# Second attention of a two-layer transformer kernel: PSUM banks shared out anew between two score passes

## The chip, the cores and the metric

The kernel runs on one core of a Trainium2 chip. It is one launch, and the metric is the device time of that launch in microseconds (us), taken as the median of several runs. The engines are TensorE (PE, with its weight loads in a row of their own, PEld), VectorE (DVE), ScalarE (ACT), GpSimd (POOL) and the queue of SyncE (SP), which issues most transfers.

## The reference, cut to what matters

The input is 16 sequences of 512 rows with 128 features. The layers are feed-forward, first attention, feed-forward, second feed-forward kind, second attention, second feed-forward kind. Only the second attention is touched by the change:

```python
B, L, C = x.shape            # 16, 512, 128
H = 16; D = C // H           # 16 heads of 8
qkv = (x @ w_qkv).reshape(B, L, 3, H, D).transpose(2, 0, 3, 1, 4)
q, k, v = (qkv[0], qkv[1], qkv[2])
q = _apply_rope(q, cos, sin)
k = _apply_rope(k, cos, sin)
attn = jnp.einsum('bhqd,bhkd->bhqk', q, k) * D ** (-0.5)
attn = jax.nn.softmax(attn, axis=-1)
out = jnp.einsum('bhqk,bhkd->bhqd', attn, v)
return out.transpose(0, 2, 1, 3).reshape(B, L, C) @ w_proj + b_proj
```

## The kernel before

A tile is one sequence: 512 rows, held as BLK = 4 blocks of 128 rows. The second attention (`attention1` on each engine, phase 4) computes the scores twice.

**Pass 1** (L2029, `pass1`) computes scores with the queries of one block as stationary operand and all 512 keys as moving operand: one 128x512 matmul for each of 4 query blocks of each of 16 heads. VectorE takes the negated maximum of each row from the PSUM bank (L1594, `maxima`). The maxima of a group of four heads are transposed (L2095, `shifted`) and added to the queries (L1600), so that the second pass gives scores with the row maximum already taken off.

**Pass 2** (L2040, `pass2`) computes the same scores transposed. One step deals with key block `h % 4` of the four heads of group `h // 4`: four 128x512 matmuls, one for each head `j` of the group. ScalarE takes the exponential out of PSUM into `prob` (L1019, `exps`). Then `values` (L2053) multiplies the exponentials with the values, four heads side by side in the array, accumulating in bank OB.

Pass 1 runs AHEAD = 5 heads before pass 2. A tile is 16 steps of h, each written out in the code of every engine (`step`), and there are 16 tiles, 256 steps in all. Nothing is reordered at run time: each engine executes its own list in order, and semaphores join the lists. `s1` counts matmuls of pass 1, `qmax` maxima, `st` finished matmuls of pass 2 and `prob` exponentials.

**TensorE's step** h before the change is: pass 2 for heads 0 and 1; `early_work`; pass 1 for block 2; pass 2 for heads 2 and 3; pass 1 for block 3; `values` of step h-1; `pass1_ahead`, which is pass 1 for blocks 0 and 1 of the next head; `late_work`. Early work is four 128x128 matmuls in steps 0, 3, 7, 11 and 15. Late work is eight 128x128 matmuls in steps 0 and 9 (L2069, L2087), three 128x512 matmuls in steps 1 and 3 (L1750 to L1752), and four 128x128 matmuls in steps 7, 8, 11, 12 and 13 (L2062, L2081). Steps 2, 4, 5, 6, 10, 14 and 15 have none. The first tile has none in steps 7 to 10 either.

**ScalarE's step** h is: `o_raw` in steps 1, 5, 9 and 13; a copy of rotated queries or keys (`qk_hl<-rope`) in steps 5 and 7; the exponentials of heads 0 and 1; two copies in step 0 and one in steps 1 and 9; the exponentials of heads 2 and 3. **VectorE's step** h is: two maxima; other work of that step (rotary products, `q_sh`, normalising the output); two maxima.

**The banks of PSUM** before the change: pass 1 uses banks 0 and 1 in turn (PASS1 + b % 2), each read by one VectorE instruction of 512 columns. Pass 2 uses banks 2 to 5 (PASS2 + j), and one ScalarE instruction reads two of them, 1024 columns. Bank 6 is OB, and bank 7 (MISC) serves everything else.

SyncE reloads `k_pad` for a group of the next tile after pass 2 has used it for the last time (L571, counted in `st`).

Of the kernel before, what the change touches and what calls it, by code (L numbers as in the profile page):

```python
# [7 lines left out]
ALU = mybir.AluOpType  # L8
# [122 lines left out]
def macaron(nc, x_in, w, const, out):  # L131
# [9 lines left out]
    with whole:  # L141
# [253 lines left out]
        PASS1, PASS2, OB, MISC = 0, 2, 6, 7  # L395
# [20 lines left out]
        def _(sp):  # L416
# [149 lines left out]
            def load_keys(t, g, again):  # L566

                if g == 0:
                    pass_wait(sp, sig(4, "k_out"), t * 48 + 64)
                if again:  # L570
                    pass_wait(sp, sig(4, "st"), t * 2 * HEADS - 2 * HEADS + 8 * g + 8)  # L571
                else:
                    pass_wait(sp, sig(4, "k_zero"), g + 1)
                for j in range(HPG):
                    sp.dma_start(k_pad[32 * j:32 * j + 3 * HD + 1, HPG * g + j, :].bitcast(F32), k_dram[HPG * g + j])\
                      .then_inc(sig(4, "k_pad"), 16)
# [40 lines left out]
            sp.wait_ge(sig(4, "st"), (TILES - 1) * 2 * HEADS + HEADS)  # L617
# [249 lines left out]
        def _(act):  # L867
# [135 lines left out]
            def attention1():  # L1003
# [12 lines left out]
                def exps(t, h, half):  # L1016
                    act.wait_ge(sig(ph, "st"), t * 2 * HEADS + 2 * h + half + 1)
                    b0 = PASS2 + 2 * half
                    act.activation(prob[:, h % HP, 2 * half:2 * half + 2, :], ps[:, b0:b0 + 2, :], ACT.Exp,  # L1019
                                   scale=SCALE).then_inc(sig(ph, "prob"), 1)  # L1020
# [70 lines left out]
        def _(dve):  # L1091
# [495 lines left out]
            def attention1():  # L1587
                ph = 4

                def maxima(t, g, j, blocks=range(BLK)):  # L1590
                    for b in blocks:
                        dve.wait_ge(sig(ph, "s1"), (t * GROUPS + g) * 16 + 4 * j + b + 1)
                        c = 32 * j + 3 * HD
                        dve.tensor_reduce(shift[:, g % 2, b, c:c + 1], wide(PASS1 + b % 2), AXX,  # L1594
                                          ALU.max, negate=True).then_inc(sig(ph, "qmax"), 1)
# [151 lines left out]
        def _(pe):  # L1747
# [266 lines left out]
            def attention1():  # L2014
# [6 lines left out]
                def pass1(t, g, j, blocks=range(BLK)):  # L2021
# [4 lines left out]
                    for b in blocks:  # L2026
                        if not (isinstance(t, int) and t == g == 0 and 4 * j + b < 2):
                            pe.wait_ge(sig(ph, "qmax"), (t * GROUPS + g) * 16 + 4 * j + b - 1)
                        pe.matmul(wide(PASS1 + b % 2), q_st[:, g % 2, b * P:b * P + P], k_pad[:, HPG * g + j],  # L2029
                                  start=True, stop=True).then_inc(sig(ph, "s1"), 1)  # L2030

                def pass2(t, h, half, first=False):

                    g, kb = h // HPG, h % HPG
                    if kb == 0 and half == 0:
                        pe.wait_ge(sig(ph, "qsh_sb"), t * GROUPS + g + 1)
                    if not first:
                        pe.wait_ge(sig(ph, "prob"), t * 2 * HEADS + 2 * h - 1 + half)
                    for j in (2 * half, 2 * half + 1):
                        last = pe.matmul(wide(PASS2 + j), k_pad[:, HPG * g + j, kb * P:kb * P + P],  # L2040
                                         q_sh[:, g % 2], start=True, stop=True)
                    last.then_inc(sig(ph, "st"), 1)

                def values(t, h, p):

                    g, kb = h // HPG, h % HPG
                    pe.wait_ge(sig(ph, "prob"), t * 2 * HEADS + 2 * h + 2)
# [112 lines left out]
                def step(t, p, h, more, before=None):  # L2160
                    first = h == 0 and before is None
# [3 lines left out]
                    pass2(t, h, 0, first)  # L2165
                    early_work(t, p, h, more, before)
                    if scores:
                        pass1(t1, g, j, (2,))
                    pass2(t, h, 1, first)
                    if scores:  # L2170
                        pass1(t1, g, j, (3,))
                    if h > 0:
                        values(t, h - 1, p)
                    elif before is not None:
                        values(before, HEADS - 1, 1 - p)
                    pass1_ahead(t, h + 1, more)
# [110 lines left out]
```

## Time and profile before

| | |
|---|---|
| median of 3 runs | 2481.73 us (2479.38 to 2483.67) |
| profiled execution, its own time | 2477.91 us |
| its span | 2476.0 us |
| PE busy | 2236.7 us, 90% of the span |
| DVE busy | 1986.3 us, 80% |
| ACT busy | 1298.4 us, 52% |
| POOL busy | 1024.6 us, 41% |
| L1594, maxima on DVE | 1024 instructions, 685 ns each |
| L1019, exponentials on ACT | 512 instructions, 1024 ns each |
| second attention, first to last matmul of its own | about 1126 to 2064 us of the span |

Busy time of PE is the sum of stretches in which a matmul is recorded as running. Matmuls are pipelined: a 128x512 matmul is recorded with some 0.39 us, while the next starts 0.23 us after it. So how fast PE goes is read from the starts of consecutive matmuls, not from their durations.

### The profile page before, as it was taken

How to read it: one execution, taken by the hardware profiler on the slowest of the kernel's cores; microseconds unless marked ns; L12 is line 12 of the kernel's file. 1: busy time of each engine (PE TensorE's matmuls, PEld its weight loads, DVE VectorE, ACT ScalarE, POOL GpSimd, SP SyncE). 2: the span in 40 equal slices, each digit the busy share in tenths (PEclk: the TensorE clock that was granted, in tenths of full speed). 3: DMA queues.
4: the chain of work that ended last, by engine and by line, in shares of the span. 5: the costliest groups of instructions: out<-in, count | busy, mean ns of one | idle time of the engine just before them, and what ended most of it. 6: DMA issues, size and time to landing. Idle time of an engine off the chain costs nothing.

```text
span 2476.0 us, 33777 instructions
## 1 busy us (share of the span) xinstructions
PE 2236.7 (90%) x11138; PEld 1544.6 (62%) x11138; DVE 1986.3 (80%) x4646; ACT 1298.4 (52%) x1907; POOL 1024.6 (41%) x953
## 2 busy tenths in 40 slices
PE   4499588779599999977999999999999999999999
PEld 3377366557377777764555555555555556777777
DVE  6588588768488888867888888888888886888887
ACT  1088333278444444433666666666666665444444
POOL 6646445536545655552211122212222203555554
PEclk9999666589789999996999999999999999999999
DMA  7243211144188887852222222222222206787887
GB/s 184 80 156 125 41 35 39 44 154 150 49 188 173 175 183 162 183 125 56 79 72 69 71 65 69 68 65 70 68 76 71 80 29 138 163 186 168 183 182 155
DMA packets 146489, 274.14 MB, mean 111 GB/s; under 512 B 21055, under 2 KB 24138, under 8 KB 146070
## 3 DMA queue, kind: packets, MB, share of 16 engines
q1 hardware_dynamic: 129942, 242.61, 41.1%
q0 software_dynamic: 16384, 29.46, 5.6%
q8 instruction: 89, 1.46, 0.3%
q14 instruction: 74, 0.61, 0.1%
HBM read 212.92 MB, written 54.65 MB: 108 GB/s over the span
## 4 chain that ended last, share of the span: by engine, by line
PE 40%; DVE 7%; DMA 5%; ACT 2%; issue 2%; SPq 0%; POOL 0%; DVEq 0%; ACTq 0%
PE ps L2029 12%; PE ps L2053 10%; PE ps L2040 9%; DMA gate_rows<-gates_dram 4%; DVE m L1429 2%; PE ps L1750 2%; DVE shift L1594 2%; PE ps L1752 2%; PE ps L1751 2%; PE ps L2062 1%; ACT hi L869 1%; PE ps L2095 1%; DMA gates_dram<-gateT 1%; DVE gate L1384 1%; PE ps L1764 1%
## 5 line engine op out<-in xcount | busy, mean ns | idle before, releaser
L1594 DVE TENSOR_REDUCE shift<-ps 128x1 fp32r<-128x512 f32 x1024 | 665.8, 685 | 132.9 <-PE ps L2029 127.2
L1019 ACT ACTIVATE prob<-ps 128x1024 f32<-128x1024 f32 x512 | 511.2, 1024 | 309.1 <-PE ps L2040 303.1
L869 ACT ACTIVATE hi<-m 128x512 fp32r<-128x512 f32 x512 | 319.0, 631 | 427.1 <-DVE m L1429 427.0
L707 POOL TENSOR_TENSOR lo<-m,hi 128x512 fp32r<-128x512 f32 x256 | 349.1, 1368 | 389.0 <-ACT hi L869 388.9
L2029 PE MATMUL ps<-k_pad,q_st 128*128 128x512 f32 x1024 | 405.2, 438 | 14.6 <-DVE shift L1594 7.2
L1429 DVE SCALAR_TENSOR_TENSOR m<-ps,gate_rows 128x512 f32<-128x512 f32 x512 | 334.8, 680 | 91.4 <-PE ps L1752 52.7
L2029 PEld LDWEIGHTS ps<-k_pad,q_st 128*128 128x128 f32 x1024 | 180.7, 190 | 271.1 <-DVE shift L1594 190.9
L2040 PE MATMUL ps<-q_sh,k_pad 128*128 128x512 f32 x1024 | 330.2, 404 | 0.0
L2053 PE MATMUL ps<-prob,v_cols 128*32 128x512 f32 x2048 | 272.7, 605 | 0.4 <-ACT prob L1019 0.4
L1096 DVE TENSOR_TENSOR lo<-m,hi 128x512 fp32r<-128x512 f32 x256 | 220.4, 861 | 16.8
L1750 PE MATMUL ps<-hi,vals_hl 128*128 128x512 f32 x512 | 211.1, 412 | 5.2 <-DVE lo L1096 4.5
L1750 PE MATMUL ps<-xnT_hl,keys_hl 128*128 128x512 f32 x512 | 210.0, 410 | 0.9 <-DVEq L382 0.9
L1751 PE MATMUL ps<-xnT_hl,keys_hl 128*128 128x512 f32 x512 | 204.2, 399 | 0.0
L1752 PE MATMUL ps<-xnT_hl,keys_hl 128*128 128x512 f32 x512 | 203.6, 398 | 0.0
L1752 PE MATMUL ps<-hi,vals_hl 128*128 128x512 f32 x512 | 203.1, 397 | 0.0
L1751 PE MATMUL ps<-lo,vals_hl 128*128 128x512 f32 x512 | 202.5, 395 | 0.0
L2040 PEld LDWEIGHTS ps<-q_sh,k_pad 128*128 128x128 f32 x1024 | 184.8, 189 | 27.0 <-ACT prob L1019 1.2
L785 POOL DMA_INDIRECT y_dram<-yb_rows,y_to x152 | 161.4, 1062 | 54.2 <-issue 54.2
L869 ACT ACTIVATE xnT<-ps 128x512 f32<-128x512 f32 x96 | 56.7, 590 | 225.1 <-PE ps L1757 121.2
L639 POOL TENSOR_SCALAR var_eps<-meanvar 128x4 f32<-128x4 f32 x48 | 11.2, 233 | 359.7 <-DVE meanvar L1653 279.0
L1096 DVE TENSOR_TENSOR g_lo<-g,g_hi 128x512 fp32r<-128x512 f32 x152 | 107.1, 705 | 35.5 <-ACT g_hi L869 30.5
L1750 PEld LDWEIGHTS ps<-hi,vals_hl 128*128 128x128 f32 x512 | 96.9, 189 | 41.0 <-DVE lo L1096 16.8
(215 smaller groups left out, 3847.9 us busy)
## 6 DMA issues: line engine op xcount, KB each, us to landing
gate_rows<-gates_dram SPq DMA_DIRECT2D x254, 512.0 KB, 12.0
w_blk<-w_dram SPq DMA_DIRECT2D x38, 514.5 KB, 3.7
q_st<-q_dram SPq DMA_DIRECT2D x64, 256.0 KB, 2.7
k_pad<-k_dram SPq DMA_DIRECT2D x256, 50.0 KB
k_dram<-qk_hl SPq DMA_DIRECT2D x48, 256.0 KB, 4.9
q_dram<-qk_hl SPq DMA_DIRECT2D x48, 256.0 KB, 3.0
x_blk<-sorted_x SPq DMA_DIRECT2D x38, 258.0 KB, 3.7
rope<-rope POOLq DMA_DIRECT2D x64, 128.0 KB, 3.3
```

Of the source, the lines that this page charges most:

```text
L707: pool.tensor_tensor(m["lo"][:, s], m["m32"][:, s], m["hi"][:, s].bitcast(F32), ALU.subtract).then_inc(sig(ph, "lo_pool"), 1)
L869: return act.activation(o, i, ACT.Copy)
L1019: act.activation(prob[:, h % HP, 2 * half:2 * half + 2, :], ps[:, b0:b0 + 2, :], ACT.Exp, scale=SCALE).then_inc(sig(ph, "prob"), 1)
L1096: return dve.tensor_tensor(o, a, b, ALU.subtract)
L1429: dve.scalar_tensor_tensor(out=m["m32"][:, fb % RING1], in0=wide(h1_bank[fb]), scalar=0.0, in1=m["gate_rows"][p][:, fb], op0=ALU.max, op1= ...
L1594: dve.tensor_reduce(shift[:, g % 2, b, c:c + 1], wide(PASS1 + b % 2), AXX, ALU.max, negate=True).then_inc(sig(ph, "qmax"), 1)
L1750: pe.matmul(dst, w_hi, x_hi, start=start, stop=False)
L1751: pe.matmul(dst, w_hi, x_lo, start=False, stop=False)
L1752: return pe.matmul(dst, w_lo, x_hi, start=False, stop=stop)
L2029: pe.matmul(wide(PASS1 + b % 2), q_st[:, g % 2, b * P:b * P + P], k_pad[:, HPG * g + j], start=True, stop=True).then_inc(sig(ph, "s1"), 1)
L2040: last = pe.matmul(wide(PASS2 + j), k_pad[:, HPG * g + j, kb * P:kb * P + P], q_sh[:, g % 2], start=True, stop=True)
L2053: last = pe.matmul(ps[rows(j), OB, :], v_cols[p][:, kb, HPG * g + j], prob[:, h % HP, j], start=(kb == 0), stop=(kb == BLK - 1))
```

## The change

Pass 1 gets four banks, 0 to 3, one for each query block (PASS1 + b). VectorE reads two neighbouring banks in one instruction and writes two maxima, so there are 512 instructions of 1024 columns instead of 1024 of 512. Pass 1 waits once for each pair of blocks: the pair may be written when the same pair of the previous head has been read. Pass 2 gets two banks, 4 and 5 (PASS2 + j % 2), where it had four. ScalarE reads one bank in each instruction, so there are 1024 exponentials of 512 columns instead of 512 of 1024. Each matmul of pass 2 for head j waits until the exponential two places before it has been taken, and `st` and `prob` now count single matmuls and single exponentials. TensorE's step changes its order: pass 1 for blocks 2 and 3 follow one another, and pass 2 for heads 2 and 3 moves behind `values`. SyncE's waits on `st` are rescaled and stand at the same point of the work.

```diff
-        PASS1, PASS2, OB, MISC = 0, 2, 6, 7
+        PASS1, PASS2, OB, MISC = 0, 4, 6, 7
...
                 def exps(t, h, half):
-                    act.wait_ge(sig(ph, "st"), t * 2 * HEADS + 2 * h + half + 1)
-                    b0 = PASS2 + 2 * half
-                    act.activation(prob[:, h % HP, 2 * half:2 * half + 2, :], ps[:, b0:b0 + 2, :], ACT.Exp,
-                                   scale=SCALE).then_inc(sig(ph, "prob"), 1)
+                    for j in (2 * half, 2 * half + 1):
+                        n = t * 4 * HEADS + 4 * h + j
+                        act.wait_ge(sig(ph, "st"), n + 1)
+                        act.activation(prob[:, h % HP, j, :], wide(PASS2 + j % 2), ACT.Exp,
+                                       scale=SCALE).then_inc(sig(ph, "prob"), 1)
...
                 def maxima(t, g, j, blocks=range(BLK)):
-                    for b in blocks:
-                        dve.wait_ge(sig(ph, "s1"), (t * GROUPS + g) * 16 + 4 * j + b + 1)
+                    for b in blocks[0::2]:
+                        dve.wait_ge(sig(ph, "s1"), (t * GROUPS + g) * 16 + 4 * j + b + 2)
                         c = 32 * j + 3 * HD
-                        dve.tensor_reduce(shift[:, g % 2, b, c:c + 1], wide(PASS1 + b % 2), AXX,
-                                          ALU.max, negate=True).then_inc(sig(ph, "qmax"), 1)
+                        dve.tensor_reduce(shift[:, g % 2, b:b + 2, c], ps[:, PASS1 + b:PASS1 + b + 2, :], AXX,
+                                          ALU.max, negate=True).then_inc(sig(ph, "qmax"), 2)
...
                     for b in blocks:
-                        if not (isinstance(t, int) and t == g == 0 and 4 * j + b < 2):
-                            pe.wait_ge(sig(ph, "qmax"), (t * GROUPS + g) * 16 + 4 * j + b - 1)
-                        pe.matmul(wide(PASS1 + b % 2), q_st[:, g % 2, b * P:b * P + P], k_pad[:, HPG * g + j],
+                        n = (t * GROUPS + g) * 16 + 4 * j + b
+                        if n >= 4 and b % 2 == 0:
+                            pe.wait_ge(sig(ph, "qmax"), n - 2)
+                        pe.matmul(wide(PASS1 + b), q_st[:, g % 2, b * P:b * P + P], k_pad[:, HPG * g + j],
...
-                def pass2(t, h, half, first=False):
+                def pass2(t, h, heads):
...
-                    if not first:
-                        pe.wait_ge(sig(ph, "prob"), t * 2 * HEADS + 2 * h - 1 + half)
-                    for j in (2 * half, 2 * half + 1):
-                        last = pe.matmul(wide(PASS2 + j), k_pad[:, HPG * g + j, kb * P:kb * P + P],
-                                         q_sh[:, g % 2], start=True, stop=True)
-                    last.then_inc(sig(ph, "st"), 1)
+                    for j in heads:
+                        n = t * 4 * HEADS + 4 * h + j
+                        if n >= 2:
+                            pe.wait_ge(sig(ph, "prob"), n - 1)
+                        pe.matmul(wide(PASS2 + j % 2), k_pad[:, HPG * g + j, kb * P:kb * P + P],
+                                  q_sh[:, g % 2], start=True, stop=True).then_inc(sig(ph, "st"), 1)
...
-                    pass2(t, h, 0, first)
+                    pass2(t, h, (0, 1))
                     early_work(t, p, h, more, before)
                     if scores:
-                        pass1(t1, g, j, (2,))
-                    pass2(t, h, 1, first)
-                    if scores:
-                        pass1(t1, g, j, (3,))
+                        pass1(t1, g, j, (2, 3))
                     if h > 0:
                         values(t, h - 1, p)
                     elif before is not None:
                         values(before, HEADS - 1, 1 - p)
+                    pass2(t, h, (2, 3))
                     pass1_ahead(t, h + 1, more)
                     late_work(t, p, h, more, before)
```

TensorE's list before the change, steps 4 and 5 of a tile in the middle of the phase (L2040 is pass 2, L2029 pass 1, L2053 `values`; the brackets name the semaphores waited for):

```order
L2040 MATMUL ps<-q_sh,k_pad 128x512 [waits prob_4,qsh_sb_4]
L2040 MATMUL ps<-q_sh,k_pad 128x512
L2029 MATMUL ps<-k_pad,q_st 128x512 [waits qmax_4]
L2040 MATMUL ps<-q_sh,k_pad 128x512 [waits prob_4]
L2040 MATMUL ps<-q_sh,k_pad 128x512
L2029 MATMUL ps<-k_pad,q_st 128x512 [waits qmax_4]
L2053 MATMUL ps<-prob,v_cols 32x512 [waits prob_4]
L2053 MATMUL ps<-prob,v_cols 32x512 x3
L2029 MATMUL ps<-k_pad,q_st 128x512 [waits qmax_4] x2
L2040 MATMUL ps<-q_sh,k_pad 128x512 [waits prob_4]
L2040 MATMUL ps<-q_sh,k_pad 128x512
```

The same place of the changed kernel, where the lines are L2043, L2031 and L2055 in the same order of meaning:

```order
L2043 MATMUL ps<-q_sh,k_pad 128x512 [waits prob_4,qsh_sb_4]
L2043 MATMUL ps<-q_sh,k_pad 128x512 [waits prob_4]
L2031 MATMUL ps<-k_pad,q_st 128x512 [waits qmax_4]
L2031 MATMUL ps<-k_pad,q_st 128x512
L2055 MATMUL ps<-prob,v_cols 32x512 [waits prob_4]
L2055 MATMUL ps<-prob,v_cols 32x512 x3
L2043 MATMUL ps<-q_sh,k_pad 128x512 [waits prob_4] x2
L2031 MATMUL ps<-k_pad,q_st 128x512 [waits qmax_4]
L2031 MATMUL ps<-k_pad,q_st 128x512
L2043 MATMUL ps<-q_sh,k_pad 128x512 [waits prob_4] x2
```

Pass 2 for heads 2 and 3 has moved behind `values`, so that two matmuls of pass 1 stand between it and the next step's pass 2, and each matmul of pass 2 now has a wait for an exponential. Before, a bank of pass 2 was written again only a whole step later.

ScalarE's list before the change, from step 1 of a tile to step 7:

```order
L869 ACTIVATE v_cols<-ps 128x64x8 [waits v_4]
L1019 ACTIVATE prob<-ps 128x1024 [waits st_4] x7
L869 ACTIVATE o_raw<-ps 128x512 [waits pv_4]
L869 ACTIVATE qk_hl<-rope 128x512 [waits k_out_4,rope_sum_4]
L1019 ACTIVATE prob<-ps 128x1024 [waits st_4] x4
```

And of the changed kernel:

```order
L869 ACTIVATE v_cols<-ps 128x64x8 [waits v_4]
L1020 ACTIVATE prob<-ps 128x512 [waits st_4] x14
L869 ACTIVATE o_raw<-ps 128x512 [waits pv_4]
L869 ACTIVATE qk_hl<-rope 128x512 [waits k_out_4,rope_sum_4]
L1020 ACTIVATE prob<-ps 128x512 [waits st_4] x8
```

The places of the other ScalarE work are the same; each exponential has become two, each with its own wait.

## Rows read from the trace of the kernel before

**Rows 1.** Busy time by stretch: start:end, length, PE, PEld, DVE, ACT, POOL, clock, DMA.

```profile
1000.00:1100.00 100.00, 92.93 (x415) 72.44 (x414) 79.16 (x174) 43.39 (x75) 51.35 (x42) 0.98 0.73 152
1115.00:1146.00 31.00, 16.79 (x33) 8.52 (x33) 21.21 (x33) 1.88 (x2) 8.25 (x10) 0.50 0.13 42
1166.00:2043.00 877.00, 872.35 (x4856) 493.64 (x4856) 750.50 (x1375) 564.66 (x644) 176.66 (x177) 1.00 0.25 68
```

**Rows 2.** Groups of instructions, 1166 to 2043 us: busy, mean ns, idle before.

```profile
L1594 DVE TENSOR_REDUCE shift<-ps 128x1 fp32r<-128x512 f32 x983 | 639.2, 686 | 124.1 <-PE ps L2029 118.5
L1019 ACT ACTIVATE prob<-ps 128x1024 f32<-128x1024 f32 x492 | 491.5, 1024 | 276.7 <-PE ps L2040 271.1
...
L2029 PEld LDWEIGHTS ps<-k_pad,q_st 128*128 128x128 f32 x984 | 170.8, 188 | 249.3 <-DVE shift L1594 176.4 <-issue 51.1
```

**Rows 3.** Timeline of PE, steps 4 and 5 of one tile: start, duration, instruction.

```profile
1447.37 0.39 PE L1750 MATMUL ps<-xnT_hl,w_qk 128*128 128x512 f32 x1
...
1448.07 0.62 PE L2040 MATMUL ps<-q_sh,k_pad 128*128 128x512 f32 x2
1448.53 0.40 PE L2029 MATMUL ps<-k_pad,q_st 128*128 128x512 f32 x1
...
1449.22 0.40 PE L2029 MATMUL ps<-k_pad,q_st 128*128 128x512 f32 x1
1449.55 1.06 PE L2053 MATMUL ps<-prob,v_cols 128*32 128x512 f32 x8
1450.54 0.72 PE L2029 MATMUL ps<-k_pad,q_st 128*128 128x512 f32 x2
1451.11 0.63 PE L2040 MATMUL ps<-q_sh,k_pad 128*128 128x512 f32 x2
1451.82 0.50 PE L2029 MATMUL ps<-k_pad,q_st 128*128 128x512 f32 x1
1452.16 0.62 PE L2040 MATMUL ps<-q_sh,k_pad 128*128 128x512 f32 x2
...
1454.55 0.63 PE L2040 MATMUL ps<-q_sh,k_pad 128*128 128x512 f32 x2
...
1457.92 0.39 PE L2040 MATMUL ps<-q_sh,k_pad 128*128 128x512 f32 x1
```

**Rows 4.** Timelines of DVE, PEld and ACT at the same steps.

```profile
1451.07 0.69 DVE L1594 TENSOR_REDUCE shift<-ps 128x1 fp32r<-128x512 f32 x1 [0.66 <-PE ps L2029]
...
1451.82 0.19 PEld L2029 LDWEIGHTS ps<-k_pad,q_st 128*128 128x128 f32 x1 [0.52 <-DVE shift L1594]
...
1448.72 1.94 ACT L1019 ACTIVATE prob<-ps 128x1024 f32<-128x1024 f32 x2 [2.03 <-PE ps L2040]
```

**Rows 5.** Shapes on ACT, whole span: busy, mean ns of one.

```profile
L896 ACT ACTIVATE g<-ps,w_blk 128x512 f32<-128x512 f32 x152 | 104.4, 687 | 25.7 <-PE ps L1752 24.2
...
L869 ACT ACTIVATE xnT_hl<-ps 128x512 fp32r<-128x512 f32 x102 | 60.1, 589 | 40.8 <-PE ps L1819 40.8
...
L869 ACT ACTIVATE o_raw<-ps 128x512 f32<-128x512 f32 x64 | 38.7, 605 | 2.6 <-PE ps L2053 1.9
```

**Rows 6.** Chain of waits, two pieces of late work: start, length, what.

```profile
1476.05 0.44 PE ps L2062 x4
...
2041.05 0.89 PE ps L2087 x8
```

**Rows 7.** Chain of waits, last steps of the phase: start, length, what.

```profile
2050.82 0.92 PE ps L2040 x4
2051.74 1.00 PE ps L2053 x8
2052.73 0.59 PE ps L2062 x4
2053.32 0.93 PE ps L2040 x4
```

**Rows 8.** ACT in step 5 (start, length), and a wait (total, times, longest).

```profile
1451.17 0.62 ACT L869 ACTIVATE qk_hl<-rope 128x512 fp32r<-128x512 f32 x1
...
ACT qk_hl L869 <- DMA rope<-rope: 31.9, 14, 2.6
```

More of the change, by code:

```diff
@@ L570, in load_keys @@
                 if again:
-                    pass_wait(sp, sig(4, "st"), t * 2 * HEADS - 2 * HEADS + 8 * g + 8)
+                    pass_wait(sp, sig(4, "st"), t * 4 * HEADS - 4 * HEADS + 16 * g + 16)
                 else:
@@ L615, in store @@
                 sp.dma_start(ov[:, bass.ds(t, 1)], xs[:, bass.ds(t, 1)]).then_inc(stored, 16)
-            sp.wait_ge(sig(4, "st"), (TILES - 1) * 2 * HEADS + HEADS)
+            sp.wait_ge(sig(4, "st"), (TILES - 1) * 4 * HEADS + 2 * HEADS)
             gates(TILES, 0)
@@ L2026, in pass1 @@
                     for b in blocks:
-                        if not (isinstance(t, int) and t == g == 0 and 4 * j + b < 2):
-                            pe.wait_ge(sig(ph, "qmax"), (t * GROUPS + g) * 16 + 4 * j + b - 1)
-                        pe.matmul(wide(PASS1 + b % 2), q_st[:, g % 2, b * P:b * P + P], k_pad[:, HPG * g + j],
+                        n = (t * GROUPS + g) * 16 + 4 * j + b
+                        if n >= 4 and b % 2 == 0:
+                            pe.wait_ge(sig(ph, "qmax"), n - 2)
+                        pe.matmul(wide(PASS1 + b), q_st[:, g % 2, b * P:b * P + P], k_pad[:, HPG * g + j],
                                   start=True, stop=True).then_inc(sig(ph, "s1"), 1)
-                def pass2(t, h, half, first=False):
+                def pass2(t, h, heads):
                     g, kb = h // HPG, h % HPG
-                    if kb == 0 and half == 0:
+                    if kb == 0 and heads[0] == 0:
                         pe.wait_ge(sig(ph, "qsh_sb"), t * GROUPS + g + 1)
-                    if not first:
-                        pe.wait_ge(sig(ph, "prob"), t * 2 * HEADS + 2 * h - 1 + half)
-                    for j in (2 * half, 2 * half + 1):
-                        last = pe.matmul(wide(PASS2 + j), k_pad[:, HPG * g + j, kb * P:kb * P + P],
-                                         q_sh[:, g % 2], start=True, stop=True)
-                    last.then_inc(sig(ph, "st"), 1)
+                    for j in heads:
[4 more added lines that the diff above has]
+                                  q_sh[:, g % 2], start=True, stop=True).then_inc(sig(ph, "st"), 1)
                 def values(t, h, p):
                     g, kb = h // HPG, h % HPG
-                    pe.wait_ge(sig(ph, "prob"), t * 2 * HEADS + 2 * h + 2)
+                    pe.wait_ge(sig(ph, "prob"), t * 4 * HEADS + 4 * h + 4)
                     if kb == 0 and not (isinstance(t, int) and t == g == 0):
@@ L2160, in step @@
                 def step(t, p, h, more, before=None):
-                    first = h == 0 and before is None
                     ahead = h + AHEAD
```

## The prediction, made before the changed kernel was run

> **What bounds the kernel now.** I read the busy time by stretch first. The change touches only the second attention, which takes some 940 of 2476 us, and in its steady part (1166 to 2043 us) PE has a matmul running for 872 of 877 us at full clock, while DVE is busy for 750 and ACT for 565 [rows 1]. The groups of instructions seem to tell another story: DVE sat idle 124 us in front of its maxima, mostly until a pass-1 matmul, and weight loads of pass 1 waited 176 us for DVE [rows 2]. Each seems to wait for the other. The timeline of PE decides it, since a weight load that waits costs nothing while an older matmul still streams. From start to start, a 128x512 matmul takes 0.23 us (the two L2040 at 1448.07, then L2029 at 1448.53). The `values` block takes 0.99 from its start to the next weight load, and that load isn't hidden, so that the pair behind it takes 0.57 instead of 0.46 to the next matmul [rows 3]. Step 4, which has neither early nor late work, is 1448.07 to 1451.11, 3.04 us, and these cadences alone fill it. So **PE's own stream is the bound**, and waits on DVE show only in places: in step 5 L2029 would be due at 1451.57 and starts its load at 1451.82, 0.06 after the end of a maximum (1451.07 + 0.69) [rows 3, 4]. That step is 3.44 long and the next, 1454.55 to 1457.92, 3.37, against 3.04 for the same work [rows 3]: 0.40 + 0.33 = 0.73 us in each tile that DVE really costs. The 176 us of [rows 2] are nearly all covered. ACT waits for pass 2 (271 us) [rows 2], it has time to spare.
>
> **What the change removes.** The matmuls are the same in number and size, so nothing leaves the bound itself. (a) With four banks, pass 1 for a pair of blocks waits for maxima of the head before, a whole step (3 us or more) old. The 0.73 us per tile go. (b) DVE saves the start of 512 instructions. No row shows a reduction of 1024 columns: it lies between 0.69 us (no more than one now) and 1.38 (twice that). Even at 1.38, DVE would need 32 x 1.38 = 44 us in a tile for maxima and (750 - 639) / 15.4 tiles = 7 us for the rest, 51 of 57 us [rows 1, 2]; I take 1.2. A reduction now starts a matmul later (0.23 us), since it waits for both banks; behind it in DVE's queue are `q_sh` and the normalising of outputs, and PE's `shifted` in steps 3, 7, 11, 15 waits for it. That reduction is fed in step h-1 and ends about 1 us ahead, so this costs nothing. (c) The head of the phase (1126 to 1147 us, clock 0.50), where pass 1 alone alternates with DVE, gets shorter by one or two us; I take 1.5.
>
> **What it adds.** Two banks instead of four for pass 2, each wait now on the exponential two places earlier. Two places follow closely on each other: pass 2 for heads 2 and 3 stands behind `values`, then come two matmuls of pass 1, then the next step's heads 0 and 1 in the same two banks. I lay this out from the weight load of pass 2 for head 2 (time 0), which comes right behind `values` and isn't hidden, as L2029 at 1450.54 now.
> - Natural starts (all waits met): head 2 at 0.11, head 3 at 0.34, pass 1 at 0.57 and 0.80, next head 0 at 1.04, next head 1 at 1.27. These are the 0.57 and 0.23 of [rows 3].
> - A matmul that starts with its own load ends 0.50 after the load (1451.82) [rows 3], and ACT follows 0.03 later (1448.07 + 0.62 to 1448.72) [rows 3, 4]. So the exponential of head 2 starts at 0.53.
> - Its length: two exponentials of 1024 take 1.94, one 1.024 [rows 2, 4], so the second starts 0.11 before the first ends. A 512-column instruction out of PSUM takes 0.589 as a copy, 0.605 as another copy, and 0.687 as the dearest [rows 5]. I take 0.60, next to the copies, since they too read 512 columns of one bank; the 0.42 that is left to 1.024 would be the price of 512 columns more. The exponential of head 3 then starts at 0.53 + 0.49 = 1.02 and ends at 1.62.
> - The load of the next head 1 follows 0.06 behind (as the load behind the maximum [rows 4]) at 1.68, the matmul 0.11 later at 1.79. It was due at 1.27: **a stall of 0.52 us**. Half of it falls on head 0 (exponential of head 2 ends 1.13, matmul 1.30 instead of 1.04), the rest on head 1.
>
> Late work stands just in this gap and covers it. Four 128x128 matmuls take 0.44, eight 0.89 [rows 6], three 128x512 take 0.70 (1447.37 to 1448.07) [rows 3]. So steps 2, 4, 5, 6, 10, 14, 15 lose 0.52 each; 7, 8, 11, 12, 13 lose 0.08; 0, 1, 3, 9 nothing. The sum in a tile: 7 x 0.52 + 5 x 0.08 - 0.73 = 3.3 us, on 57.
>
> The other pair is safe: heads 2 and 3 need the exponentials of heads 0 and 1, with two matmuls of pass 1 and `values` between, 2.1 us from head 0 to head 2 against 0.93 at the tight place. ACT has other work ahead of the exponentials in steps 5 and 7, where a copy waits up to 2.6 us for a transfer [rows 8]; that eats this margin and may add 0.2 us in a tile, which I leave in the range. ACT's load itself stays below the bound: 64 x 0.49 + (565 - 492) / 15.4 = 36 us of 60 [rows 1, 2]. SyncE's reload of `k_pad` waits for the last matmul of pass 2 in a group, which now ends some 1 us later in its step; it is needed seven steps later.
>
> **The total.** Tiles 1 to 14: 14 x 3.3 = 46. Tile 0, which has its own mix of late work and DVE waits, I count like the others: about 3. In the last tile pass 1 is absent from step 11 on, so nothing but the 0.44 of late work stands between the tight pair. Now a step there is 2.50 us (2050.82 to 2053.32) [rows 7]; the gap is 0.46 shorter and the cover 0.44, so steps 11 to 14 lose about 0.54 and the very last 1.0; with 5 x 0.52 + 2 x 0.08 - 0.73 = 2.0 for the steps before, and 0.3 for the last `values`, which waits for two exponentials more, about 5.5 for that tile. The head gives back 1.5. 46 + 3 + 5.5 - 1.5 = **53 us**, 2477.9 + 53 = 2531 for an execution like the profiled one. The median of the runs is 3.8 above it, so **2535**.
>
> **Bounds of the one unknown.** The stall moves by twice the change of the exponential's length. At 0.687, the dearest row, it is 0.69: 7 x 0.69 + 5 x 0.25 - 0.73 = 5.4 a tile, about +86, 2568. The cheapest possible is half of 1.024, 0.51: stall 0.34, 7 x 0.34 - 0.73 = 1.7 a tile, about +29, 2511. The Trainium skill's page "ScalarE: Activation LUTs", section "What ACT_TABLE_LOAD costs", gives an instruction with constant scale and bias 186 ns and 0.833 ns a column, overlapping the next by 93 ns. For 1024 columns that is 1.039, and the trace has 1.024, so it nearly agrees; for 512 it would be an estimate of 0.613 and a spacing of 0.52, by which the sum were some 8 us larger. The row-based value stands.
>
> **Rivals.**
> 1. *DVE is the true partner of the bound, and the exponentials hide* (faster). The 0.73 us in 15 tiles and the head would be gained, 11 + 1.5, and nothing lost: 2469. It decides by the exponential: the chain 0.50 + 0.03 + 2e - 0.11 + 0.17 must be below 1.27, so e below 0.34 us. No row of [rows 5] is near. Were the weights loaded ahead of the wait, the stall would shrink by 0.11 only. Chance 0.05.
> 2. *The stalls bring the clock down.* Most steps then have two gaps of about 0.26 us. Where PE was busy 17 of 31 us the clock was 0.50, its 1.2 GHz level; at 93 of 100 it was 0.98 [rows 1]. After the change PE would be busy for about 94%. If a twentieth of the phase ran at half clock, that costs 45 us: 2580. "TensorE: Matmul & The Clock Gate" of the Trainium skill, section "A second HAM failure mode: psum-queue depth-cycling", describes just such short idle spells from the cycling of PSUM banks, with a clock that swings. The trace gives it little support: gaps of 0.3 us in steps 5 and 6 left it at 1.00. Chance 0.04.
> 3. *Single exponentials are dearer than 0.687, or ACT's waits for transfers fall on the shorter cover*: 0.5 us more in 10 steps of each tile is 80 us: 2600. Chance 0.04.
> 4. *The stalls are as said but partly shared*: where one step is late, the next has its inputs ready, and the loss is below half: about 2500. For it speaks that waits of the trace overlap elsewhere; against it, that both ends of the chain, pass 2 behind `values` and the next pass 2, lie on PE itself. Chance 0.07, of which a quarter ends within 0.2%.
>
> **How the numbers follow.** The forecast, a loss between 2511 and 2568 by the bounds, has 0.80, most of it near 2535. Slower by over 0.2% (5 us, about what a measurement of this kernel can tell): 0.80 + 0.04 + 0.04 + 0.05 = 0.93; within: 0.02; faster: 0.05. The range for 8 in 10 is 2513 to 2562.
>
> **What would show it.** In the profile of the changed kernel the weight loads of pass 2 should name ACT's exponentials as their releaser, seven times a tile about 0.5 us; steps without late work should be 3.56 long instead of 3.04, and steps 5 and 6 3.56 instead of 3.44 and 3.37; a tile 60.4 instead of 57.1; the exponentials 0.60, the reductions about 1.2 and with no PE waits behind them; the clock 1.00. It would be wrong if the pass-2 loads don't wait (rival 1), if the exponential isn't near 0.60 (the size), if the clock dips (2), or if heads 2 and 3 wait behind `values` (3).

## The result and the profile after

The changed kernel takes 2544.0 us in the median (2541.13 to 2547.1, 4 runs) against 2482.7 for the kernel before (2479.38 to 2488.39, 4 runs): a ratio of 1.0244, 95% interval 1.0229 to 1.0259. It is **61 us slower** (57 to 64). I had forecast 53 us more, a time of 2535 with a range of 2513 to 2562.

The busy time by stretch of the changed kernel (columns as in [rows 1]) answers the last row of that group:

```profile
1166.00:2043.00 877.00, 871.03 (x4558) 454.79 (x4557) 673.86 (x816) 566.18 (x1064) 174.27 (x175) 1.00 0.25 67
```

PE seems as busy as before and the clock is at 1.00, its 2.4 GHz level, but in the same 877 us it gets 4558 matmuls done where it had 4856. DVE has 77 us less to do. Here busy time tells nothing: a matmul that waits for the load of its weights is recorded as running (the pair at 1480.47 below has 0.98 us, where the pair at 1477.27 has 0.62).

The groups of instructions between 1166 and 2095 us (busy, mean ns of one, idle before and its releaser) show who is waited for now; they answer [rows 2]:

```profile
L1595 DVE TENSOR_REDUCE shift<-ps 128x2 fp32r<-128x1024 f32 x489 | 597.7, 1223 | 208.8 <-PE ps L2031 208.3 <-issue 0.2
L1020 ACT ACTIVATE prob<-ps 128x512 f32<-128x512 f32 x978 | 531.9, 598 | 304.8 <-PE ps L2043 296.8
...
L2031 PEld LDWEIGHTS ps<-k_pad,q_st 128*128 128x128 f32 x976 | 178.0, 189 | 31.5
L2043 PEld LDWEIGHTS ps<-q_sh,k_pad 128*128 128x128 f32 x978 | 162.1, 188 | 307.0 <-ACT prob L1020 239.1 <-issue 57.8
```

One exponential of 512 columns takes 598 ns (I had taken 600), one reduction of 1024 columns 1223 ns (I had taken 1200). The loads of pass 1 no longer wait for DVE at all, and those of pass 2 wait 239 us for ACT. As with the 176 us of [rows 2], most of that is covered by older matmuls that are still running. What it costs is read from the starts of matmuls. Steps 4 and 5 of a tile on PE, which answer [rows 3] (start, duration):

```profile
1477.27 0.62 PE L2043 MATMUL ps<-q_sh,k_pad 128*128 128x512 f32 x2
1477.73 0.62 PE L2031 MATMUL ps<-k_pad,q_st 128*128 128x512 f32 x2
1478.29 1.07 PE L2055 MATMUL ps<-prob,v_cols 128*32 128x512 f32 x8
1479.28 0.74 PE L2043 MATMUL ps<-q_sh,k_pad 128*128 128x512 f32 x2
1479.86 0.63 PE L2031 MATMUL ps<-k_pad,q_st 128*128 128x512 f32 x2
1480.47 0.98 PE L2043 MATMUL ps<-q_sh,k_pad 128*128 128x512 f32 x2
1481.30 0.63 PE L2031 MATMUL ps<-k_pad,q_st 128*128 128x512 f32 x2
...
1484.04 0.99 PE L2043 MATMUL ps<-q_sh,k_pad 128*128 128x512 f32 x2
```

Two matmuls in a row take 0.46 us from the first start to the next instruction (1477.27 to 1477.73). The pair at 1480.47 takes 0.83, and it begins 0.15 late (1479.86 + 0.46 = 1480.32). Together that is 0.52 us lost, at one place of the step. Step 5 is 1480.47 to 1484.04, 3.57 us, where the work alone takes 3.04. The timelines of ACT and PEld at the same place show the chain link by link:

```profile
1479.82 1.09 ACT L1020 ACTIVATE prob<-ps 128x512 f32<-128x512 f32 x2 [1.04 <-PE ps L2043]
...
1480.47 0.19 PEld L2043 LDWEIGHTS ps<-q_sh,k_pad 128*128 128x128 f32 x1 [0.42 <-ACT prob L1020]
1480.96 0.19 PEld L2043 LDWEIGHTS ps<-q_sh,k_pad 128*128 128x128 f32 x1 [0.30 <-ACT prob L1020]
```

Counted from the load of pass 2 for head 2 at 1479.28, the exponentials start at 0.54 and both are done at 1.63, and the load that needs the second starts at 1.68. My layout had 0.53, 1.62 and 1.68.

The 0.52 us lie across the boundary of two steps: 0.15 ahead of the next step's head 0, 0.37 behind it. So a step is 3.56 long only where the gap ahead of it and the gap behind it both stall, as in steps 5 and 6. Steps 2 and 4, which follow late work, have 3.20 in the trace, step 10 has 3.28 and step 14 3.38. I had written 3.56 for all of them; the sum over a tile isn't touched by this.

### The profile page after: what moved, and what is told of

Read it like the earlier page. It is cut to its first block, busy times and chain, and to the rows that moved or that the text cites. A ratio compares the mean times of both kernels' runs of the same rounds, so it can differ in the third digit from the quotient of the medians.

```text
span 2544.1 us, 34288 instructions
## 1 busy us (share of the span) xinstructions
PE 2288.6 (90%) x11138; PEld 1531.0 (60%) x11138; DVE 1951.1 (77%) x4134; ACT 1338.5 (53%) x2419; POOL 1025.2 (40%) x953
## 4 chain that ended last, share of the span: by engine, by line
PE 38%; DMA 8%; DVE 5%; ACT 3%; issue 2%; POOL 1%; SPq 0%; DVEq 0%; ACTq 0%
PE ps L2043 12%; PE ps L2055 8%; PE ps L2031 8%; DMA gate_rows<-gates_dram 4%; DMA rope<-rope 3%; DVE m L1430 2%; PE ps L1751 2%; PE ps L1753 2%; PE ps L1752 2%; PE ps L2064 1%; ACT hi L869 1%; DMA gates_dram<-gateT 1%; PE ps L2097 1%; ACT prob L1020 1%; POOL qk_hl L664 1%
## 5 line engine op out<-in xcount | busy, mean ns | idle before, releaser
L1595 DVE TENSOR_REDUCE shift<-ps 128x2 fp32r<-128x1024 f32 x512 | 625.2, 1222 | 217.5 <-PE ps L2031 217.1
L1020 ACT ACTIVATE prob<-ps 128x512 f32<-128x512 f32 x1024 | 556.9, 598 | 339.1 <-PE ps L2043 330.9
L2043 PE MATMUL ps<-q_sh,k_pad 128*128 128x512 f32 x1024 | 406.7, 460 | 6.7 <-ACT prob L1020 5.1
L2043 PEld LDWEIGHTS ps<-q_sh,k_pad 128*128 128x128 f32 x1024 | 170.4, 188 | 320.3 <-ACT prob L1020 250.5
L2031 PE MATMUL ps<-k_pad,q_st 128*128 128x512 f32 x1024 | 332.2, 406 | 9.3 <-DMA k_pad<-k_dram 5.5
L2055 PE MATMUL ps<-prob,v_cols 128*32 128x512 f32 x2048 | 272.7, 605 | 1.0 <-ACT prob L1020 0.9
L2031 PEld LDWEIGHTS ps<-k_pad,q_st 128*128 128x128 f32 x1024 | 189.0, 192 | 47.3 <-issue 7.4
```

Source lines behind the costliest of these rows:

```text
L1020: act.activation(prob[:, h % HP, j, :], wide(PASS2 + j % 2), ACT.Exp, scale=SCALE).then_inc(sig(ph, "prob"), 1)
L1595: dve.tensor_reduce(shift[:, g % 2, b:b + 2, c], ps[:, PASS1 + b:PASS1 + b + 2, :], AXX, ALU.max, negate=True).then_inc(sig(ph, "qmax"), 2)
L2031: pe.matmul(wide(PASS1 + b), q_st[:, g % 2, b * P:b * P + P], k_pad[:, HPG * g + j], start=True, stop=True).then_inc(sig(ph, "s1"), 1)
L2043: pe.matmul(wide(PASS2 + j % 2), k_pad[:, HPG * g + j, kb * P:kb * P + P], q_sh[:, g % 2], start=True, stop=True).then_inc(sig(ph, "st"), 1)
L2055: last = pe.matmul(ps[rows(j), OB, :], v_cols[p][:, kb, HPG * g + j], prob[:, h % HP, j], start=(kb == 0), stop=(kb == BLK - 1))
```

## The experiments

All of them are edits of the changed kernel. "A tile" is the distance between the first matmuls of pass 2 of two following tiles, read from the trace in the middle of the phase. The runs were shared out over several chips, on which the kernel before had medians of 2474, 2480 and 2483 us, so kernels are compared by their ratio to the kernel before on the same chip.

| kernel | ratio | 95% interval | a tile, us |
|---|---|---|---|
| before | 1 | | 57.1 |
| the change | 1.0244 | 1.0229 to 1.0259 | 60.9 |
| e1, single exponentials alone | 0.9989 | 0.9977 to 1.0002 | 57.1 |
| e2, single maxima | 1.0230 | 1.0203 to 1.0257 | 60.8 |
| e3, late work out of the gap | 1.0472 | 1.0444 to 1.0501 | 64.5 |
| e4, three banks each | 1.0049 | 1.0033 to 1.0065 | 58.0 |
| e5, interleaved order | 1.0132 | 1.0116 to 1.0147 | 59.4 |
| e6, exponentials of half the columns | 1.0046 | 1.0031 to 1.0061 | 58.0 |
| e7, second copy one step later | 1.0204 | 1.0189 to 1.0220 | 60.4 |
| e8, e4 + e5 + e7 | 0.9973 | 0.9961 to 0.9985 | 56.6 |
| e9, new order, old banks | 1.0251 | 1.0232 to 1.0270 | 60.7 |
| e10, new banks, old order | 1.0625 | 1.0600 to 1.0650 | 67.1 |

### Which part of the change costs?

**e1** keeps only the smaller exponentials:

```diff
-        PASS1, PASS2, OB, MISC = 0, 4, 6, 7
+        PASS1, PASS2, OB, MISC = 0, 2, 6, 7
-                        if n >= 2:
-                            pe.wait_ge(sig(ph, "prob"), n - 1)
-                        pe.matmul(wide(PASS2 + j % 2), ...
+                        if n >= 4:
+                            pe.wait_ge(sig(ph, "prob"), n - 3)
+                        pe.matmul(wide(PASS2 + j), ...
```

Maxima, pass 1 and TensorE's order are those of before.

> One part of the change alone: exponentials of one bank each (1024 of 512 columns) and counts of single matmuls, but pass 2 keeps four banks, pass 1 keeps two banks with single maxima, and TensorE keeps the order of before. My theory says that small exponentials cost nothing in themselves, since ScalarE has time to spare and a bank is used again only a whole step later: a tile 57.1 us as before, time within 5 us of the kernel before (2477 to 2487). The rival that the doubled number of exponentials and semaphore waits is what costs says at least half of the loss, 2512 or more.

It runs like the kernel before, 0.9989, and a tile is 57.1 us. Twice as many exponentials and waits cost nothing in themselves. They bring nothing either: the Trainium skill's page "Perfetto Trace Analysis", section "Optimizing Scalar/DVE Operations", says that breaking up instructions of an engine that isn't saturated but causes gaps elsewhere may let work finish sooner. Here ACT caused no gap before, and e1, the one run that changes this alone, shows no gain.

**e2** takes the maxima one block at a time again, in the four banks of the change:

```diff
-                    for b in blocks[0::2]:
+                    for b in blocks:
...
-                        dve.tensor_reduce(shift[:, g % 2, b:b + 2, c], ps[:, PASS1 + b:PASS1 + b + 2, :], AXX,
-                                          ALU.max, negate=True).then_inc(sig(ph, "qmax"), 2)
+                        dve.tensor_reduce(shift[:, g % 2, b, c:c + 1], wide(PASS1 + b), AXX,
+                                          ALU.max, negate=True).then_inc(sig(ph, "qmax"), 1)
```

> The changed kernel with its maxima taken by single instructions of 512 columns again, each with its own wait; banks, order and exponentials stay. My theory says that VectorE is off the path, so 1024 instructions of 0.69 us instead of 512 of 1.22 change nothing: 2544 within 5 us, a tile 60.9. If the wide instruction, which starts one matmul later, costs anything, this one is faster by more than 5 us; if the saved instruction starts are worth something, slower, by up to 64 x 0.07 = 4.5 us a tile, 70 us.

1.0230 against 1.0244: the intervals overlap, and a tile is 60.8 against 60.9. The headline of the change, maxima of two blocks in one instruction, neither costs nor gains anything that these runs can tell.

**e9 and e10** separate order and banks. e9 has the change's order with two banks for pass 1 (single maxima) and four for pass 2 (single exponentials). e10 has the change's banks with the order of before:

```diff
                     if scores:
-                        pass1(t1, g, j, (2, 3))
+                        pass1(t1, g, j, (2,))
+                    pass2(t, h, (2, 3))
+                    if scores:
+                        pass1(t1, g, j, (3,))
...
-                    pass2(t, h, (2, 3))
                     pass1_ahead(t, h + 1, more)
```

> The other part alone: the change's order on TensorE (pass 1 for blocks 2 and 3 together, pass 2 for heads 2 and 3 behind values), with the banks of before (two for pass 1 with single maxima, four for pass 2) and single exponentials. With four banks pass 2 never waits, so my theory says that the order costs nothing there. But with two banks four matmuls of pass 1 now come in two close pairs, and the second of blocks 2 and 3 needs the maximum of block 1: blocks 0 and 1 are at 0.57 and 0.80 of the layout, their maxima (0.60 apart, then 0.69) end 1.2 to 1.9 later, block 3 is due at 1.97. A step without other work is about 3.3 to 3.6, a tile about 60.6, 52 to 59 us above the kernel before, now with weight loads of pass 1 waiting for VectorE. If the order cost nothing at all, 2480 as before.

> The banks, waits and instructions of the change with TensorE's order of before: pass 2 for heads 2 and 3 now comes two or three matmuls behind heads 0 and 1, instead of behind values. By the same layout the tight pair is then heads 0, 1 and 2, 3: head 2 is due 0.70 after head 0 and may start 1.20 after it (matmul 0.40, 0.03, exponential 0.60, load 0.17), head 3 about 0.26 later still, in all steps but those with early work in this gap: about 0.75 lost in 11 steps of 16 and 0.3 in five, a tile 66 to 68, 143 to 162 us above the kernel before. If what the change costs is its order, this runs like the kernel before or at least faster than the change.

e9 is 2.5% slower, 60.7 us a tile. The loss is just as large as in the change, but it sits on the other pass. These are the loads of e9 in steps 4 and 5:

```profile
1481.69 0.42 PEld L2044 LDWEIGHTS ps<-q_sh,k_pad 128*128 128x128 f32 x2
1482.63 0.19 PEld L2032 LDWEIGHTS ps<-k_pad,q_st 128*128 128x128 f32 x1 [0.52 <-DVE shift L1596]
1483.23 0.19 PEld L2032 LDWEIGHTS ps<-k_pad,q_st 128*128 128x128 f32 x1 [0.41 <-DVE shift L1596]
```

Pass 2 loads its two weights without a gap, and pass 1 waits for two maxima, 0.60 us apart. e10 is 6.25% slower, 155 us, within the 143 to 162 expected. This is TensorE in a step of e10 behind late work:

```profile
1477.83 0.70 PE L2043 MATMUL ps<-q_sh,k_pad 128*128 128x512 f32 x2
1478.37 0.40 PE L2031 MATMUL ps<-k_pad,q_st 128*128 128x512 f32 x1
1478.99 0.99 PE L2043 MATMUL ps<-q_sh,k_pad 128*128 128x512 f32 x2 [0.23 <-ACT prob L1020]
1479.82 0.39 PE L2031 MATMUL ps<-k_pad,q_st 128*128 128x512 f32 x1
```

Heads 2 and 3 are due at 1478.60, come 0.39 late and take 0.83 instead of 0.46: 0.76 lost, where 0.75 was laid out. So neither the banks nor the order can be called the cause alone: **each of the two belongs to the other**. The order of before spreads pass 1 and has pass 2 in one close group, which loses with two banks (e10) and not with four (e1). The order of the change spreads pass 2 better and has pass 1 in close pairs, which lose with two banks (e9) and not with four. With two banks for pass 2 the new order is the better one by far, and it still loses.

### Is the stall in the gap, and is it the chain that I laid out?

**e3** moves the late work out of the gap between pass 2 for heads 2, 3 and the next heads 0, 1:

```diff
+                    late_work(t, p, h, more, before)
                     pass2(t, h, (2, 3))
                     pass1_ahead(t, h + 1, more)
-                    late_work(t, p, h, more, before)
```

> The changed kernel with the late work moved ahead of pass 2 for heads 2 and 3, out of the gap between that and the next step's heads 0 and 1. The work is the same. My theory says that late work covers the stall in 9 steps of 16; moved, all 16 steps lose 0.52: 4 x 0.52 for steps 0, 1, 3, 9 and 5 x 0.44 for 7, 8, 11, 12, 13 more, 4.3 us a tile, less what steps 0 and 7 lost already to ScalarE's other work: a tile 64.5 to 65.2, time about 2600 to 2615. If the stall is not in this gap (the order of values and pass 2 as such, or the number of waits), the time stays within 10 us of 2544.

64.5 us a tile, 4.72% above the kernel before (117 us; the change 61): some 56 more for moving matmuls past each other. A tile was expected at 64.5 to 65.2, so this is the low end. In the timeline of e3 step 1 has its three matmuls of late work ahead of the pair, and the next pair of pass 2 now waits:

```profile
1474.28 0.50 PE L1751 MATMUL ps<-xnT_hl,w_qk 128*128 128x512 f32 x1
1474.62 0.40 PE L1752 MATMUL ps<-xnT_hl,w_qk 128*128 128x512 f32 x1
1474.85 0.39 PE L1753 MATMUL ps<-xnT_hl,w_qk 128*128 128x512 f32 x1
1475.08 0.62 PE L2043 MATMUL ps<-q_sh,k_pad 128*128 128x512 f32 x2
1475.54 0.63 PE L2031 MATMUL ps<-k_pad,q_st 128*128 128x512 f32 x2
1476.16 0.99 PE L2043 MATMUL ps<-q_sh,k_pad 128*128 128x512 f32 x2
1476.99 0.62 PE L2031 MATMUL ps<-k_pad,q_st 128*128 128x512 f32 x2
```

1475.54 to 1476.16 to 1476.99: 0.62 + 0.83 instead of 0.46 + 0.46, a loss of 0.53 in a step that lost nothing in the change.

**e4** gives each pass three banks. Pass 1 takes bank n % 3 with single maxima, each matmul waiting for the maximum three places before it, and pass 2 likewise:

```diff
-        PASS1, PASS2, OB, MISC = 0, 4, 6, 7
+        PASS1, PASS2, OB, MISC = 0, 3, 6, 7
-                        if n >= 2:
-                            pe.wait_ge(sig(ph, "prob"), n - 1)
-                        pe.matmul(wide(PASS2 + j % 2), ...
+                        if n >= 3:
+                            pe.wait_ge(sig(ph, "prob"), n - 2)
+                        pe.matmul(wide(PASS2 + n % 3), ...
```

> The changed kernel with three banks for each pass instead of four and two: maxima of single blocks, exponentials of one bank, each bank used again three matmuls later, TensorE's order as in the change. By my layout of the tight pair the next head 1 then needs the exponential of head 2, which ends at 1.13 instead of 1.62, matmul at 1.30 against 1.27 due: the stall of 0.52 shrinks to 0.03. Left are waits of pass 1 on maxima and step 7's wait for a transfer: a tile 57.5 to 58.5, time 2485 to 2505. If the loss came from the order (pass 2 behind values) or from the single exponentials, it stays near 2544.

1.0049, 58.0 us a tile. In its timeline the pair of pass 2 behind two matmuls of pass 1 is all but free of waits:

```profile
1450.64 0.63 PE L2032 MATMUL ps<-k_pad,q_st 128*128 128x512 f32 x2
1451.11 0.65 PE L2044 MATMUL ps<-q_sh,k_pad 128*128 128x512 f32 x2
1451.60 0.72 PE L2032 MATMUL ps<-k_pad,q_st 128*128 128x512 f32 x2
```

The pair starts 0.47 after the one before and takes 0.49: 0.04 lost, where the layout had 0.03. One bank more for pass 2 takes the stall of 0.52 away. What is left above the kernel before is step 7, which is 5.03 us in this tile against 3.86: without it a tile would be some 56.8, below the 57.5 to 58.5 that I expected. More on that below.

**e5** keeps the banks of the change and interleaves the two passes one matmul at a time:

```diff
-                    pass2(t, h, (2, 3))
-                    pass1_ahead(t, h + 1, more)
+                    pass2(t, h, (2,))
+                    pass1_ahead(t, h + 1, more, (0,))
+                    pass2(t, h, (3,))
+                    pass1_ahead(t, h + 1, more, (1,))
```

and likewise pass 2 for heads 0 and 1 with pass 1 for blocks 2 and 3.

> The changed kernel, same banks and instructions, with pass 2 and pass 1 of a step interleaved one by one: pass 2 head 0, pass 1 block 2, pass 2 head 1, early work, pass 1 block 3, values, pass 2 head 2, pass 1 block 0 of the next head, pass 2 head 3, pass 1 block 1, late work. In my layout head 2 stays at 0.11 and its exponential ends at 1.13, the next head 0 is still due at 1.04 and starts at 1.30; head 3 is at 0.57, its exponential ends at 1.62, the next head 1 starts at 1.79 but is now due at 1.50 (1.76 after head 0's delay). The stall falls from 0.52 to 0.29. A step without late work is 3.33, the 0.08 of the steps with 0.44 of late work goes: a tile 58.4 plus step 7's wait for the transfer (0.3 to 1.1), 58.7 to 59.5, time 24 to 36 us above the kernel before. If the number of banks alone decides, the time stays at 2.3 to 2.5% above.

1.0132 (33 us), 59.4 us a tile. Step 5 begins like this:

```profile
1465.97 0.40 PE L2031 MATMUL ps<-k_pad,q_st 128*128 128x512 f32 x1
1466.36 0.50 PE L2043 MATMUL ps<-q_sh,k_pad 128*128 128x512 f32 x1
1466.69 0.40 PE L2031 MATMUL ps<-k_pad,q_st 128*128 128x512 f32 x1
1466.93 0.41 PE L2043 MATMUL ps<-q_sh,k_pad 128*128 128x512 f32 x1
```

0.39 and 0.33 instead of 0.23 twice: the wait falls on head 0 only and is 0.26, and head 1 finds its exponential all but done. Steps 5 and 6 are 3.34 us long on average, where 3.33 was laid out.

**e6** leaves out half of the work of each exponential (256 of 512 columns; the rest of `prob` stays at one):

```diff
-                        act.activation(prob[:, h % HP, j, :], wide(PASS2 + j % 2), ACT.Exp,
+                        act.activation(prob[:, h % HP, j, 0:256], ps[:, PASS2 + j % 2, 0:256], ACT.Exp,
```

> The changed kernel with each exponential taken over half of its columns (256 of 512; the other half of the tile keeps ones, so the output is not the reference's). The exponential takes about 0.39 us instead of 0.60, spaced 0.27. The chain counts it twice: the stall falls by about 0.43, from 0.52 to 0.09, and only in the seven steps without late work. A tile is then 57.1 plus at most 1.5 (0.6 for the seven steps, up to 1.2 for step 7's wait for a transfer, minus 0.73 of waits on maxima): 57.0 to 58.6, time 0 to 24 us above the kernel before. If the length of the exponential isn't in the chain (the waits or the order as such cost), the time stays at 2.3 to 2.5% above.

1.0046, 58.0 us a tile. The exponential takes 382 ns, and two of them 0.66 us; step 5 is 1458.34 to 1461.47, 3.13 us, where the layout says 3.04 + 0.09:

```profile
1457.83 0.66 ACT L1021 ACTIVATE prob<-ps 128x256 f32<-128x256 f32 x2 [1.47 <-PE ps L2044]
...
1458.34 0.71 PE L2044 MATMUL ps<-q_sh,k_pad 128*128 128x512 f32 x2
...
1461.47 0.71 PE L2044 MATMUL ps<-q_sh,k_pad 128*128 128x512 f32 x2
```

0.22 us less for each exponential took 0.43 off the step: its length counts twice, as two of them lie between the tight pairs. Step 7 is 4.89 on average here, 1.0 above the kernel before. That is more than the whole 0.9 by which a tile is longer. The 0.1 that is left of each stall is outweighed by the waits on DVE that went, and what e6 still loses is step 7.

### What step 7 costs

The sum had 3.3 us a tile, the trace has 3.8 (60.9 against 57.1). Step 7 stands out in the change, and the chain of waits of the changed kernel through it shows why (start, length, what):

```profile
1482.01 1.28 POOL qk_hl L664
1483.29 0.52 POOL rope L659
1483.81 5.73 DMA rope<-rope
1489.55 0.02 issue
1489.57 0.63 ACT qk_hl L869
1490.20 0.49 ACT prob L1020
1490.69 0.04 issue
1490.74 0.99 PE ps L2043 x2
```

The second transfer of rotated rows is issued by POOL behind a subtraction (L664), which itself waits for ACT's first copy in step 5. It lands at 1489.55, and ACT, which executes in order, has stood in front of it for 1.53 us with the exponentials of step 7 behind. Pass 2 for head 2, due at 1490.40 behind `values`, comes at 1490.73, and since head 3 waits for its exponential too, the pair takes 0.82 (to 1491.56) instead of 0.57: 0.58 us in all. Before the change ACT waited longer for the same transfer [rows 8], but pass 2 had four banks, and the wait didn't reach PE.

**e7** moves that copy on ACT:

```diff
-                    if h in (5, 7) and more:
-                        rope_high(n, q, (h - 5) // 2)
+                    if h in (5, 8) and more:
+                        rope_high(n, q, (h - 5) // 3)
```

> The changed kernel with ScalarE's second copy of rotated rows (qk_hl<-rope) in step 8 instead of step 7. In the trace of the change step 7 is 4.78 us where my layout had 4.44, since this copy waits 1.5 us for a transfer in front of the exponentials of heads 0 and 1, and pass 2 for head 2 waits for these. Moved one step later the transfer has landed: step 7 is 4.44, a tile 60.55 instead of 60.9, 5 us faster than the change in all (about 55 above the kernel before). If the excess of step 7 has another cause, nothing changes.

A tile is 60.36, 0.54 less, and the ratio 1.0204 against 1.0244: about 10 us. The direction is as expected; the size is above the 5 that I had written, since I had taken only part of the excess for this wait (step 7 is 4.22 now, not 4.44). With it gone, a tile lies 3.26 us above that of the kernel before, and the sum of the prediction said 3.3.

**e8** puts together what the runs had shown: three banks for each pass (e4), the interleaved order (e5) and the later copy (e7).

> Three banks for each pass (as in the run with three banks), the interleaved order, and ScalarE's second copy in step 8. With three banks the step without late work was 3.05 and its only large loss was step 7 (5.03 us, 1.2 over its natural length), which waited for the transfer. Without that wait a tile should be 56.6 to 56.9 against 57.1 of the kernel before, as pass 1 with three banks also loses part of its waits on maxima: 3 to 9 us faster than the kernel before. If moving the copy only moves the wait to step 8, it stays 8 to 14 us slower.

0.9973, interval 0.9961 to 0.9985: **8 us faster than the kernel before**, 2471.7 against 2479.7. It has the lowest ratio of all; its interval touches that of e1, but a tile is 56.6 against 57.1 there. The copy finds its transfer landed and runs between exponentials without idle time:

```profile
1463.07 1.09 ACT L1020 ACTIVATE prob<-ps 128x512 f32<-128x512 f32 x2 [1.42 <-PE ps L2044]
1464.04 0.64 ACT L869 ACTIVATE qk_hl<-rope 128x512 fp32r<-128x512 f32 x1
1464.56 1.09 ACT L1020 ACTIVATE prob<-ps 128x512 f32<-128x512 f32 x2
```

The gain is some 0.5 us a tile of the 0.73 of waits on maxima that the change had reached for. Of the rest 0.20 stays in step 5 (3.24 instead of 3.04), where `values` comes late. With this order of work little more was to be had, since PE's own stream is some 56.4 us of each tile's 57.1 (57.1 less the 0.73).

## Why the prediction was right, and where it was off

The mechanism held, step by step. Without step 7's wait (e7), steps 4 to 7 of a tile, averaged over the phase, are 0.84 us longer together than those of the kernel before; the sum has 3 x 0.52 - 0.73 = 0.83 for them.

- *PE's stream is the bound, and the 176 us of waits on DVE are nearly all covered.* Right: in e8 the loads of pass 1 wait 2.5 us for DVE in the same stretch, and 8 us came back, not 176. e2 shows that in the banks of the change the form of DVE's maxima doesn't matter.
- *The 0.73 us a tile of real waits on DVE go.* Right: no load of pass 1 waits for DVE in the steady part of the change. It is about the whole of what there was to gain.
- *The tight pair of pass 2 stalls 0.52 us.* Right to 0.01 us, in the links and in the sum. e3 (where the gap is), e4 (one bank more), e5 (order within the gap), e6 (length of the exponential) and e10 (the pair in another place) each moved the stall by the amount that the layout gives, within some 0.03 us where a single stall is read.
- *Late work covers it in 9 steps of 16.* Right: e3 took the cover away.
- *The exponential of 512 columns takes 0.60.* Measured 0.598. The Trainium skill's page "ScalarE: Activation LUTs", section "What ACT_TABLE_LOAD costs", had given an estimate of 0.613 with a spacing of 0.52; the trace has two in 1.09, a spacing of 0.49.
- *ACT's wait for the transfer in steps 5 and 7 may add 0.2 us, left in the range.* **This was the term that was mis-sized.** It is 0.54 us a tile by e7, some 8 us of the phase. With it the sum is 61, which is what was measured; that this fits to the microsecond is partly luck, as the next point says. I had seen the wait [rows 8] and that it used up cover, but had counted it at nothing, since it cost nothing before. It was a wait behind four banks then, and behind two now, and what counts is how much lateness of ACT the banks let through. The transfer itself takes as long as before: from the end of ACT's first copy to the start of its second there are 7.5 to 8.1 us in the kernel before and 7.3 to 8.0 in the change. So shorter steps ahead of it only make the wait longer. In e4 and e6 step 7 is 5.1 and 4.9 us on average, against 4.85 in the change.
- *The last tile and the head.* In the profiled executions the head is 2.8 us shorter (I had 1.5), tile 0 3.5 longer (3), tiles 1 to 14 54 (46), and the last tile 3.3 (5.5): 58 us in all, against 53. So two small terms that were off the other way hide some of step 7. No run was made for them, and why the last tile loses less is open. The medians are 61 us apart; where the other 3 us lie is not shown, and they are within the interval. The first matmul of pass 1 started at 1137.8 us in the profiled execution of the change and at 1125.8 in that of before, 12 us that lie in parts which the change doesn't touch. It goes with the chip: 1124 to 1128 in e1 to e4, 1132 to 1136 in e5 to e8, 1137 to 1138 in e9 and e10, each group on one chip. Single profiled executions are therefore compared by the length of the phase, not by their whole time.
- *The rivals.* DVE as the true partner (1) needed exponentials below 0.34 us; e6 with 0.38 had still 0.1 us too much in steps 5 and 6. The clock (2) stayed at 1.00 in the steady part of the change. Of all runs only e10, the slowest, shows it at 0.50 there (1.2 GHz), once, for 3.4 us from 1522.4 on. Just before, ACT had waited 2.55 us for a transfer in step 7, and PE had stood idle for 1.33 us up to 1521.35. At the lower level one `values` block took 1.87 us instead of 0.99, and the tile took 69.3 us where most others took about 67. One case doesn't show a cause, and the short stalls of the change left the clock alone. Dearer exponentials or transfers (3) was right in its second half, at a tenth of its price. Shared stalls (4) did not occur: with step 7's wait gone a tile is 3.26 us longer, as summed.

## What to carry to other kernels

Where one engine's own stream is the bound, count for each buffer how much of that stream lies between two uses, and compare it with the whole way through the other engine: end of the write, the reader's instructions, the wait and the first weight load. An engine that is busy only two thirds of the time, as ACT here, may still need all its buffers, because they are its only slack in distance. A wait on a third party that costs nothing today is priced by the depth that hides it: when that depth is cut, price it anew.

## What the runs showed of the hardware

The way through the small `values` matmuls (128x32 weights) costs PE some 0.2 us each time: 0.32 to 0.33 instead of 0.23 ahead of them and 0.34 instead of 0.23 behind them, by the load that isn't hidden. The kernel before shows it [rows 3], and where nothing else waits so do all the others. The page "TensorEngine Tiling (Array Packing)" of the Trainium skill, section "Key Properties", says that a change of tiling mode drains TensorE; the trace agrees, with these numbers.

On DVE, one reduction over two banks takes 1223 ns, where two over one bank each take 1.28 to 1.29 us together, so the wider form saves only 0.07 us of a pair. One alone takes 0.685, but the second of two starts 0.60 after the first, which hides part of its fixed cost already. On ACT, an exponential out of PSUM took 382, 598 and 1024 ns at 256, 512 and 1024 columns.
